# A two-layer attention and mixture-of-experts kernel: the second layer's 1024-wide hidden rows are transposed in f32 and split into f16 high and low parts where they leave PSUM

## The reference, cut to what matters

```python
def absmax_quant(x):
    gamma = jnp.max(jnp.abs(x), axis=-1, keepdims=True)
    x_hat = jnp.clip(x * Q_B / gamma, -Q_B + EPS, Q_B - EPS)
    return x_hat * gamma / Q_B
...
def bitlinear(x, w):
    xn = layer_norm(x)
    x_hat = xn + jax.lax.stop_gradient(absmax_quant(xn) - xn)
    w_hat = w + jax.lax.stop_gradient(ternarize_weights(w) - w)
    return jnp.einsum('bsd,od->bso', x_hat, w_hat)
```

## Time and profile before

| | |
|---|---|
| Runs | 541.4, 544.52, 545.48 us, median 544.52 |
| Profiled execution, span | 538.6 us |
| Busy share PE / DVE / ACT / POOL | 73% / 64% / 42% / 61% |
| Layer 1's loop | from about 375 us to the end |
| POOL L475 `low`, 16 instructions | 34.1 us, 2151 ns each |

### The profile page before, as it was taken

The page is one execution under the profiler, slowest core; times in us unless marked ns, Lnnn a source line. Parts: engine busy times, 40 slices in busy tenths (PEclk is TensorE's granted clock), DMA queues, the critical chain, the costliest instruction groups (busy, mean ns, idle before and its releaser), DMA issues.

```text
span 538.6 us, 7310 instructions
## 1 busy us (share of the span) xinstructions
PE 395.6 (73%) x2243; PEld 293.0 (54%) x2243; DVE 343.5 (64%) x899; ACT 228.4 (42%) x516; POOL 326.7 (61%) x300
## 2 busy tenths in 40 slices
PE   0999507969879888786888789656578776778673
PEld 0964203648656676565666767553245544556462
DVE  5549998425433644544373352682999999999950
ACT  1344105135335434333343334515657565767641
POOL 3520009054668787888888874802469779668872
PEclk9999957999788989989799798879879888989887
DMA  8800201695998878878778756600000000000001
GB/s 264 271 1 0 71 27 52 180 299 127 256 240 198 195 171 173 190 150 194 173 175 172 136 68 121 231 1 1 0 1 1 21 2 19 21 4 17 21 21 38
DMA packets 59480, 57.95 MB, mean 108 GB/s; under 512 B 7643, under 2 KB 57139, under 8 KB 59443
## 3 DMA queue, kind: packets, MB, share of 16 engines
q1 hardware_dynamic: 42643, 34.16, 21.1%
q0 software_dynamic: 12288, 18.88, 18.8%
q10 hardware_dynamic: 4512, 4.46, 2.4%
HBM read 39.72 MB, written 17.76 MB: 107 GB/s over the span
## 4 chain that ended last, share of the span: by engine, by line
DVE 33%; PE 27%; DMA 16%; issue 10%; POOL 10%; ACT 3%; SPq 1%; POOLq 0%; ACTq 0%; DVEq 0%
DMA W<-tok_d,idxE 7%; DMA acc_d<-W,idxE 5%; DVE W L1128 4%; POOL acc_d L432 4%; DVE F L921 3%; PE two L1363 3%; PE two L1323 3%; DVE nv L1107 3%; PE two L1232 3%; POOL F L417 2%; PE two L1198 2%; PE two L1289 2%; POOL W L410 2%; DVE nv L1108 2%; DMA F<-tok_d,idxE 2%
## 5 line engine op out<-in xcount | busy, mean ns | idle before, releaser
L432 POOL DMA_INDIRECT acc_d<-W,idxE x64 | 101.7, 1589 | 30.8 <-DVE W L958 14.6
L410 POOL DMA_INDIRECT W<-tok_d,idxE x56 | 56.5, 1008 | 35.1 <-DVE idxE L947 18.3
L638 ACT ACTIVATE W<-two 128x256 f32<-128x256 f32 x64 | 24.5, 383 | 84.4 <-PE two L1352 84.3
L958 DVE TENSOR_SCALAR W<-two,W 128x256 f32<-128x256 f32 x56 | 27.0, 482 | 50.4 <-PE two L1375 42.0
L981 DVE SCALAR_TENSOR_TENSOR W<-W,two 128x88 f32<-128x88 f32 x64 | 15.7, 245 | 58.1 <-ACT W L654 57.5
L1352 PE MATMUL two<-ident,W 128*128 128x128 f32 x112 | 26.3, 318 | 28.9 <-DMA W<-tok_d,idxE 26.7
L1323 PE MATMUL two<-A,v 128*128 128x128 f32 x256 | 37.7, 309 | 12.8 <-DVE A L912 7.0
L1323 PEld LDWEIGHTS two<-A,v 128*128 128x128 f32 x256 | 35.8, 224 | 15.3 <-issue 14.9
L417 POOL TENSOR_TENSOR F<-F,tid 128x512 f16<-128x512 f16 x6 | 12.6, 2132 | 50.8 <-DVE F L921 50.8
L1352 PEld LDWEIGHTS two<-ident,W 128*128 128x128 f32 x112 | 19.7, 203 | 41.8 <-DMA W<-tok_d,idxE 35.5
L1460 PE MATMUL two<-wfcT,F 128*128 128x512 f16 x128 | 34.7, 420 | 7.4 <-ACT W L700 7.4
(11 more groups left out here) (227 smaller groups left out, 1075.8 us busy)
## 6 DMA issues: line engine op xcount, KB each, us to landing
acc_d<-xn ACTq DMA_DIRECT2D x8, 512.0 KB, 4.1
W<-in_L_ffn_w_gate SPq DMA_DIRECT2D x20, 176.0 KB
W<-in_L_ffn_w_up SPq DMA_DIRECT2D x20, 176.0 KB
W<-in_L_ffn_w_down SPq DMA_DIRECT2D x20, 176.0 KB
F<-in_L_ffn_w_gate SPq DMA_DIRECT2D x12, 176.0 KB
F<-in_L_ffn_w_up SPq DMA_DIRECT2D x12, 176.0 KB
F<-in_L_ffn_w_down SPq DMA_DIRECT2D x12, 176.0 KB
x<-in_L_attn_q SPq DMA_DIRECT2D x4, 512.0 KB, 6.2
```

The lines of the kernel that those rows point to most:

```text
L410: pool.indirect_dma_start(out=xg[n % XR], out_offset=None, in_=tok_d[:, :], in_offset=bass.IndirectOffsetOnAxis(ap=idxE[:, n:n + 1], axis=0))\
L432: pool.indirect_dma_start(out=acc_d[n % 2][:, :], out_offset=bass.IndirectOffsetOnAxis(ap=idxE[:, n:n + 1], axis=0), in_=ysb[n % YS], in_o ...
L638: sc.activation(xgT[n % 2], bk_(2)[:, 0:D].rearrange("p (k n) -> p k n", k=KH), ACT.Copy)\
L958: ve.tensor_scalar(ysb[n % YS], bk_(3)[:, 0:D], xg[n % XR][:, D + n:D + n + 1], 0.5, ALU.mult, ALU.mult)\
```

## The change

`hi16`, `lo16`, VectorE's casts and GpSimd's `low` go. VectorE's two clips (L1131) now signal `hq_ready` themselves. PE transposes the f32 rows straight from `hid`, eight blocks a row tile instead of sixteen, into both banks of `two[2]`. ACT copies these 1024 f32 columns once into `hiT` as f16; VectorE's new `low_hidden(n)` subtracts `hiT` from the same PSUM columns into `loT`. Two calls of `low_hidden` enter VectorE's iteration, one behind `spreads(p)` and one behind `means(p+1)`. `gelu(n)` waits for the transposes of row tile n - 4 (`hT1_ps`) instead of their subtraction, `turn_hidden` for `loT_ready` of the row tile before, `down1` for its own. No DMA changes.

```diff
--- before.py
+++ after.py
@@ -192,8 +192,6 @@
 
         hiT = [l1(512).bitcast(F16) for _ in range(2)]
         loT = [l1(512).bitcast(F16) for _ in range(2)]
-        hi16 = [l1(512).bitcast(F16) for _ in range(GT)]
-        lo16 = [l1(512).bitcast(F16) for _ in range(GT)]
         xq = [l1(GT * D).rearrange("p (q d) -> p q d", q=GT) for _ in range(2)]
         qT_hi = l1(GT * D // 2).bitcast(F16).rearrange("p (q k n) -> p q k n", q=GT, k=KH)
         qT_lo = l1(GT * D // 2).bitcast(F16).rearrange("p (q k n) -> p q k n", q=GT, k=KH)
@@ -272,9 +270,9 @@
             sem(n) for n in ("scale_ready", "qkv_ps", "qkv_ready", "prod_ready", "dif_ready", "td_ready", "att0_ready",
                              "att_ready", "attT_ps",
                              "attT_ready", "s1_ps", "s1_ready")]
-        fc_ps, gelu_ready, nmean_ready, sq_ready, zhalf_ready, hi_ready, lo_ready, hT1_ps, hT1_ready = [
+        fc_ps, gelu_ready, nmean_ready, sq_ready, zhalf_ready, hq_ready, hT1_ps, hiT_ready, loT_ready = [
             sem(n) for n in ("fc_ps", "gelu_ready", "nmean_ready", "sq_ready", "zhalf_ready",
-                             "hi_ready", "lo_ready", "hT1_ps", "hT1_ready")]
+                             "hq_ready", "hT1_ps", "hiT_ready", "loT_ready")]
         z_ps, ztanh_ready, zu_ready, out_ready, out_stored = [sem(n) for n in (
             "z_ps", "ztanh_ready", "zu_ready", "out_ready", "out_stored")]
 
@@ -470,11 +468,6 @@
                                         .to_broadcast([P, NKV1, REP1, HD1]), ALU.mult))
                 pool.tensor_tensor(att_h[1], att_h[1], heads(mid), ALU.add).then_inc(att_ready, 1)
 
-            def low(n):
-                pool.wait_ge(hi_ready, n + 1)
-                pool.tensor_tensor(lo16[n % GT], hid[n // GT % 2][:, n % GT, :], hi16[n % GT], ALU.subtract)\
-                    .then_inc(lo_ready, 1)
-
             def finish(n):
 
                 q_, t = n % GT, n // GT + NP * (n % GT)
@@ -500,9 +493,6 @@
                     add_gated(p + 3)
                 if p + 1 < NP:
                     score_products(p + 1)
-                if p < NP:
-                    for q_ in range(GT):
-                        low(GT * p + q_)
 
         @block.scalar
         def _(sc):
@@ -696,7 +686,7 @@
                 sc.wait_ge(scale_ready, 2 * (n // GT) + 2)
                 sc.wait_ge(fc_ps, n + 1)
                 if n >= 2 * GT:
-                    sc.wait_ge(lo_ready, n - 2 * GT + 1)
+                    sc.wait_ge(hT1_ps, n - 2 * GT + 1)
                 sc.activation(hid[n // GT % 2][:, q_, :], two[1][:, :], ACT.Gelu, scale=fcscale[n // GT % 2][:, q_:q_ + 1],
                               accum_out=hsum[:, q_:q_ + 1]).then_inc(gelu_ready, 1)
 
@@ -710,8 +700,7 @@
                 sc.wait_ge(hT1_ps, n + 1)
                 if n >= 2:
                     sc.wait_ge(z_ps, n - 1)
-                sc.activation(hiT[n % 2], bk_(4).bitcast(F16), ACT.Copy).then_inc(hT1_ready, 1)
-                sc.activation(loT[n % 2], bk_(5).bitcast(F16), ACT.Copy).then_inc(hT1_ready, 1)
+                sc.activation(hiT[n % 2], two[2][:, :], ACT.Copy).then_inc(hiT_ready, 1)
 
             def own_value(p):
 
@@ -1128,13 +1117,12 @@
                     last = mark(ve.tensor_scalar(h, h, hscale[:, q_:q_ + 1], hbias[:, q_:q_ + 1], ALU.mult, ALU.add))
                 ve.wait_ge(dve, last)
                 for h in rows:
-                    last = mark(ve.tensor_scalar(h, h, QB, -QB, ALU.min, ALU.max))
-
-                if p:
-                    ve.wait_ge(hT1_ps, GT * p)
-                for q_, h in enumerate(rows):
-                    ve.wait_ge(dve, last - GT + 1 + q_)
-                    ve.tensor_copy(hi16[q_], h).then_inc(hi_ready, 1)
+                    ve.tensor_scalar(h, h, QB, -QB, ALU.min, ALU.max).then_inc(hq_ready, 1)
+
+            def low_hidden(n):
+
+                ve.wait_ge(hiT_ready, n + 1)
+                ve.tensor_tensor(loT[n % 2], two[2][:, :], hiT[n % 2], ALU.subtract).then_inc(loT_ready, 1)
 
             def silu2(n):
                 p, q_ = n // GT, n % GT
@@ -1165,6 +1153,8 @@
                 if p < NP:
                     score_difference(p)
                     spreads(p)
+                if 1 <= p <= NP:
+                    low_hidden(GT * (p - 1))
                 if p + 2 < NP:
                     moments(p + 2)
                 if p < NP:
@@ -1174,6 +1164,8 @@
                     silu(p + 3)
                 if p + 1 < NP:
                     means(p + 1)
+                if 1 <= p <= NP:
+                    low_hidden(GT * (p - 1) + 1)
                 if p < NP:
                     quantise_hidden(p)
                 if p + 2 < NP:
@@ -1481,17 +1473,15 @@
                 ins.then_inc(s1_ps, 1)
 
             def turn_hidden(n):
-                pe.wait_ge(lo_ready, n + 1)
+                pe.wait_ge(hq_ready, n + 1)
                 if n:
-                    pe.wait_ge(hT1_ready, 2 * n)
-                for b, part in ((4, hi16), (5, lo16)):
-                    for k in range(FF1 // P):
-                        ins = pe.transpose(bk_(b).bitcast(F16)[:, P * k:P * k + P], part[n % GT][:, P * k:P * k + P],
-                                           ident16[:, :])
+                    pe.wait_ge(loT_ready, n)
+                for k in range(FF1 // P):
+                    ins = pe.transpose(two[2][:, P * k:P * k + P], hid[n // GT % 2][:, n % GT, P * k:P * k + P], ident[:, :])
                 ins.then_inc(hT1_ps, 1)
 
             def down1(n):
-                pe.wait_ge(hT1_ready, 2 * n + 2)
+                pe.wait_ge(loT_ready, n + 1)
                 if n >= GT:
                     pe.wait_ge(zu_ready, n // GT * GT)
                 i = 0
```

## The result

The changed kernel takes 576.6 us (median of 4 runs, 576.03 to 577.7) against 544.32 us (four runs of the kernel before): 1.060 times as long, 95% interval 1.055 to 1.065. The forecast was 570, slower, 553 to 586.

A forecast was written before the change was run, and what follows sets the result against it. VectorE was taken to bound the kernel; a stage summed to 25.0 us, five stages +27.2, opening -1.5, end 0: +25.7 on 538.6 gives 564.3, plus 5.9 carried over, 570 us; 8 in 10 within 553 to 586.

The forecast's parts named there:

- (a): Stage, from the end of `low_q` until the first exit can start: 8.0 us, bounds 6.4 and 9.1.
- (b): Stage, the first exit, VectorE's 1024-column subtraction from PSUM: 1.13 us.
- (e): Stage, the second exit, VectorE's 1024-column subtraction from PSUM: 1.13 us.
- (c): Stage, VectorE after the first exit, from moments to the quantised rows ready: 4.56 us.
- (d): Stage, from quantised rows through PE's transposes, gelu and ACT's copies to the second exit: 5.5 us, bounds 5.2 and 7.2.
- (f): Stage, VectorE's four wide operations after the second exit: 3.85 us, bounds 3.2 and 5.3.
- (g): Stage's last part on VectorE, product scales and `low_q`: 0.8 us.
- Rival A: PE falls behind as well, delaying the next stage's `qkv`: stage 28 us, total 585 us; chance 0.12.
- The end: Stages 6 and 7 to the last `down1`: +4.1 us to the wide operations' end, -4.1 behind it, cancelling.
- The opening: Stage 0, which has no exits and loses its two casts: -1.5 us.
- From span to time: Whole kernel: predicted span 564.3 us, plus the 5.9 us by which the earlier median exceeded its profiled span.
- Rival C: Faster, if `hiT` is there when `spreads` ends: stages -0.5 us each, total -9, 535.5 us; chance 0.08.

The follow-up runs named there:

- tail_silu: Changed kernel with, in the last two iterations only, VectorE's `silu2` of the pair before ahead of the second exit; 573.1 us, ratio 1.058 to the kernel before.
- early_turn: Changed kernel with only PE's and ACT's order changed: both rows' transposes and `hiT` copies come earlier; 532.7 us, ratio 0.980 to the kernel before.
- early_first: Changed kernel with only the first row's transposes ahead of `qkv` and its copy behind `half_tanh`; 546.6 us, ratio 0.999 to the kernel before.

## Why the prediction was right, step by step

**The mechanism held.** The exit waits in VectorE's queue for a copy behind gelu, `fc` and `qkv` of the same stage, and gelu waits for transposes of the same stage. The stage sum said 25.0 us; measured 25.2. Its terms, over stages 1 to 5 or in the stage at 446.3:

| term | predicted | measured |
|---|---|---|
| (a) to the first exit | 8.0 | 7.8 mean, 6.65 to 8.8 |
| (b), (e) an exit | 1.13 | 1.14 |
| (c) to the quantised rows | 4.56 | 4.4 |
| (d) to the second exit | 5.5, high end 7.2 | 7.0 (6.8 in one stage) |
| (f) wide operations | 3.85, low end 3.2 | 2.8 in four stages, 3.7 in one |
| (g) scales, `low_q` | 0.8 | 0.8 |

Two terms were mis-sized and nearly cancelled, which is luck. (d): PE does all of `turn_q`, `turn_att` and the transposes at half clock, 3.7 us instead of 2.0; "part may run at half clock" was too mild after an idleness of 4.7 us that the sum itself implied. (f): GpSimd, without its two subtractions and released by the longer stage, is through with all but its last small operation when the wide operations of this stage begin; I had reckoned with that for L447 alone.

**PE as a second bound.** Rival A happened in part: `qkv` starts 0.1 to 2.4 us after the end of `low_q`, and the chain runs over `project` and `down1`; the sign that `fc` would start no later after `low_q` than before did not hold. It did not add its 3 us to every stage, since PE, busy without a gap from `project` to `fc`, is back at full clock for `qkv` (1.31 us in the chain), which gives most of the lateness back. The sum adds VectorE's path; where PE is late, the chain takes PE's from the transposes on, and the lateness shows in the next (a): 8.8 us where PE is 2.3 late, 6.65 where it is 0.2 late, at full clock. The 8.0 of the sum had another ground, half clock at the head of the stage; only stage 1 ran so (8.1). That the mean came out at 7.8 is thus luck as well.

**The end was the wrong step.** I had +4.1 to the end of the last wide operations and -4.1 behind it, 0 in all; measured +5.8. From the last `low_q` to the end of the wide operations the changed kernel takes 31.8 us and the one before 26.8, so +5.0. Behind them I had 8.6 us to the last `down1`, with half of its matmuls hidden; it is 13.6. So the sum was off by 0.9 up to there and by 5.0 behind. The cause of the 5.0 is a wait that I left out: `down1` of a pair's first row waits for `zu_ready`, and `silu2`, which gives it, is queued behind the second exit. tail_silu shows it, 5.0 us.

**The opening**: -1.2 for -1.5.

**From span to time.** The sum was 7.1 us short for layer 1 (+25.7 against +32.8), and the 570 some 6.5 short of the median. Between the two lie errors that nearly offset each other by chance: the 5.9 us carried over from span to median was 4.4 too much, since the changed kernel's median lies 1.5 above its span, and the profiled execution had 3.6 us more ahead of the code that changed.

**Rival C's price**, -9 without a wait, was about right in total only: early_turn is 10.7 us faster in layer 1 (153.8 against 164.5). Its stages gain 1.8, not 0.5: the exits cost 0.8 more than the casts, L1108 gives 1.2, and, not in the sum, L1040 and L1053 give 0.6 and the wide operations 0.8. Its end gains only 0.6, not the 4.1 of the sum. On contention the rule cited from the Trainium skill (GPSIMD Engine Reference, section 1, Specifications) agrees with the trace: L1108 took 1.50 us with `low` beside it and 0.15 without, though no run shows whether it ran in a two-port mode. And the exit, which has one PSUM and one SBUF input, takes 1.22 us whether GpSimd is busy beside it or not, on which that rule and the rows agree too. The transposes: eight take 1.04 us, so the 275 ns of the Trainium skill (TensorE: Matmul & The Clock Gate, Part 4: PE-mode transpose) do not add up, as the rows had it. One f32 transpose took 0.27 us at full clock, close to the figure of the Trainium skill, which is for bf16, and each started 0.11 us behind the one before.

## What to carry to other kernels

Before moving an operation into the queue of the engine that bounds the kernel, follow its input back to the instruction that releases it: if that instruction is the bounding engine's own last one of the stage before, the engine stands idle in every stage until the round trip is over (3.9 to 6.2 us here), however cheap the operation. The cure here was not the old code but the order of the other queues: the hidden rows were ready at 445.5 us here, and PE fetched them at 449.5 and 460.3. And when a producer moves behind another instruction, list who else is queued there; `silu2` cost 5 us that no busy time showed.

## What the runs showed of the hardware

- Idle time on PE also costs after it has ended. With 4.66 us of idleness ahead, four f32 transposes took 1.12 us instead of 0.60, the eight behind them 1.91 instead of 1.04, and `project`, behind 2.35 us more, 3.78 instead of 1.99; with dummy matmuls in both gaps the granted clock stayed at 1.00, and the stages became 12.8 of their 126.1 us shorter. The length of the last gap does not tell the clock by itself: in early_first, with the same 2.35 us ahead of `project` and under 1.6 ahead of `turn_q`, it took 1.99 us in two of five stages and 3.4 to 3.6 in three.
- Eight 128x128 transposes in f32 take what sixteen in f16 took (1.04 and 1.06 us at full clock), and ACT's copy of 1024 f32 columns from PSUM what that of 1024 f16 columns took (1.01 us).
- A 128x2 operation on VectorE took ten times its 0.15 us when GpSimd was in the middle of a 2.1 us one (L1108: 455.68 to 457.18, `low` until 457.15). VectorE's subtraction from PSUM, 1024 columns, took 1.22 us with or without GpSimd beside it.
